# An embedding stage rewritten: centred query/key weights, one product for their norm, the embedding norm on ScalarE and the score shift inside the exponential

## The chip, the cores and the metric

The kernel runs on one core of one Trainium2 chip. The metric is the device time of one execution in microseconds (us). Names of engines are those of the profile: PE is TensorE (PEld its weight loads), DVE is VectorE, ACT is ScalarE, POOL is GpSimd, SP is SyncE, which here only issues DMAs.

## What is computed

One layer for 8 batches of 1024 tokens, width 128. For each token a row of a table is fetched (64 numbers of a fine embedding, 64 cluster logits), the logits go through a softmax and a small product, and both halves make `h`. Then attention with 8 heads, where queries and keys are normed, and a feed-forward part with a router. Cut to what the change touches:

```python
fine_emb = fine_embed_w[location_ids]
cluster_logits = loc_to_cluster_w.T[location_ids] + loc_to_cluster_b
cluster_dist = jax.nn.softmax(cluster_logits, axis=-1)
coarse_emb = jnp.einsum('bsc,ch->bsh', cluster_dist, coarse_embed_w)
h = jnp.concatenate([fine_emb, coarse_emb], axis=-1)
xn = _ln(_layernorm(h))             # two norms, one after the other
q = silu(xn) @ w_q + b_q            # k and v alike
q = _ln(q, g_q, be_q)               # k alike; (y - mean) * rsqrt(var + eps) * g + b
q = q * inner ** (-0.5)
# softmax attention over q, k, v, then the output product and the feed-forward part
```

## The kernel before

Three stages follow one another, each a block of its own with a barrier between: `embed` (about the first 254 us of the profiled execution), `attend` and `finish`. The change is in `embed` alone.

`embed` works on chunks of 512 tokens (4 tiles of 128). Four chunks, called ways, make a round, and there are four rounds (`ITERS`). Every buffer in SBUF exists once per way. The accumulators in PSUM exist twice (`SLOTS`): `psA` for transposes, `psV` for the coarse product and the values, `psQK` for queries and keys; ways 0 and 2 share one, 1 and 3 the other. Each engine runs its own list of instructions strictly in the order written by hand, and waits on semaphores that count ways. Lines below are those of the profile of before. What happens to one way:

- POOL copies the indices (L319) and issues four gathers of 128 table rows (L322), `gather`.
- ACT copies the fine half (L551). DVE adds the cluster bias (L380), finds the negated maximum (L385) and adds it (L389), all in `logits`; ACT takes the exponential of the whole way at once (L556); DVE sums it (L396, L399).
- PE transposes the exponentials (L653), ACT copies them out (L561), PE makes the coarse product (L665), DVE divides it by the sum into `h` (L407, `coarse_half`).
- DVE: mean and variance of `h` (L417, L423, L428, `stats_front`); POOL: the root (L339, `root_front`, by a power); DVE: the norm, four instructions (L435, `norm_front`); ACT: tanh (L566); DVE: silu (L443); PE transposes (L675), ACT copies out (L571, `copy_silu_t`).
- PE: bias and product with the weights (L138, L691, L696, `project`). ACT copies queries and keys from PSUM to SBUF (L578) and the values (L583), both in `copy_projected`.
- DVE: mean and variance of queries and keys (L451, L459, L462, `stats_back` and `aggregate_back`); POOL: the root (L346, `root_back`); DVE norms the queries (L468, L473, `norm_back`), ACT the keys (L591, `norm_k`), 4 instructions each.
- PE transposes them into `psQK` (L711); ACT applies gain and shift (L600) and rounds to a first bfloat16 part (L606), both in `scale_qk`; POOL subtracts that part (L354, `subtract_part0`); ACT rounds the second (L611, `round_rest`); DVE subtracts for the third (L480, `subtract_part1`). SP stores the parts, the values and `h`, and loads the first stacks for `attend`.

A round mixes two stages of the pipeline: the queries and keys of round `it` and the embedding of round `it + 1`, while POOL gathers for round `it + 2`. All rounds but the last run in a hardware loop (`Fori`) on each engine. A fifth set of gathers, for a round that does not exist (indices set to 0), is issued too, since the loop body is always the same. `regather` waits for all four ways of the round before. The work of the last round for ways 0 and 1 is split by DVE alone (L536, L538, L540).

## Time and profile before

| | us |
|---|---|
| runs of the kernel | 1194.0, 1194.92, 1200.92 (median 1194.92) |
| the profiled execution, own time | 1192.67 |
| its span | 1190.9 |
| DVE busy over the span | 983.6 (83%) |
| PE busy | 1019.2 (86%) |
| ACT busy | 762.0 (64%) |
| POOL busy | 220.5 (19%) |

The median is the number to compare with. The profiled execution is one run of the same program; the span is from its first to its last instruction, and 1.8 us lie around it. Busy time counts instructions of an engine, not whether anyone waits for them, so the stages have to be read one by one.

### The profile page before, as it was taken

What the parts mean: (1) busy time and instruction counts of PE and PEld (TensorE: products, weight loads), DVE (VectorE), ACT (ScalarE), POOL (GpSimd) and SP (SyncE); (2) the same over time, 40 slices, a digit from 0 to 9 for tenths busy, and PEclk for the clock granted to TensorE, in tenths of its full rate; (3) what the DMA queues carried; (4) which work ended last, traced back from release to release, by engine and by line L of the source; (5) the groups of instructions that cost most, each with busy time, mean ns of one, the idle gap of its engine ahead of it and who ended that gap; (6) DMA issues with size and microseconds to landing.
All of it is one profiled execution on the core that took longest, in us unless ns stands there. A gap on an engine that the chain in (4) does not pass through costs nothing. (4 is left out here: it accounts for less than half of the span.)

```text
span 1190.9 us, 30565 instructions
## 1 busy us (share of the span) xinstructions
PE 1019.2 (86%) x12144; PEld 537.1 (45%) x12144; DVE 983.6 (83%) x2004; ACT 762.0 (64%) x1414; POOL 220.5 (19%) x321
## 2 busy tenths in 40 slices
PE   0586674749999999999999999999999849897978
PEld 0474563612434444444444344444444225856556
DVE  4679798868899889989999989989898357879794
ACT  0357665722787788888888788888878935152432
POOL 6776858330000000000000000000000010202020
PEclk9976775755999999999999999999999987989899
DMA  3232857780243242432424233242300241313011
GB/s 71 69 106 95 177 124 89 159 211 7 38 79 51 41 89 38 64 66 49 81 38 73 57 55 56 58 72 38 72 12 12 89 135 38 97 53 115 8 35 36
DMA packets 81841, 85.04 MB, mean 71 GB/s; under 512 B 24241, under 2 KB 58614, under 8 KB 81718
## 3 DMA queue, kind: packets, MB, share of 16 engines
q1 hardware_dynamic: 70710, 73.87, 28.3%
q0 software_dynamic: 2560, 5.25, 3.3%
q10 hardware_dynamic: 8448, 4.20, 1.2%
q8 instruction: 88, 1.44, 0.5%
q14 instruction: 35, 0.29, 0.1%
HBM read 48.78 MB, written 34.08 MB: 70 GB/s over the span
## 5 line engine op out<-in xcount | busy, mean ns | idle before, releaser
L1089 DVE TENSOR_REDUCE b_neg_max<-psM 128x1 f32<-128x1024 f32 x512 | 603.3, 1220 | 67.3 <-PE psM L987 64.1
L1061 ACT ACTIVATE prob<-psS 128x512 f32<-128x512 f32 x1024 | 529.1, 604 | 157.5 <-PE psS L1007 157.5
L987 PE MATMUL psM<-ks,qs 96*32 96x512 bf16 x4096 | 416.0, 394 | 18.2 <-PEq L850 14.4
L1007 PE MATMUL psS<-qs,ks 99*32 99x512 bf16 x4096 | 404.9, 382 | 6.5 <-ACT prob L1061 4.5
L1021 PE MATMUL psO<-prob,vs 128*17 128x512 f32 x2048 | 266.4, 592 | 0.2 <-ACT prob L1061 0.2
L1007 PEld LDWEIGHTS psS<-qs,ks 99*32 99x32 bf16 x4096 | 114.0, 96 | 208.4 <-ACT prob L1061 103.1
L987 PEld LDWEIGHTS psM<-ks,qs 96*32 96x32 bf16 x4096 | 113.4, 97 | 176.9 <-DVE b_neg_max L1089 83.4
L882 POOL CAST mpart<-b_neg_max 128x16 bf16<-128x16 f32 x32 | 6.3, 196 | 635.1 <-DVE b_neg_max L1089 622.0
L322 POOL DMA_INDIRECT emb<-in_table,idx x80 | 79.5, 994 | 34.0 <-issue 18.3
L1021 PEld LDWEIGHTS psO<-prob,vs 128*17 128x17 f32 x2048 | 59.5, 98 | 52.0 <-ACT prob L1061 1.1
L1285 ACT ACTIVATE y_t<-c_psT 128x512 f32<-128x512 f32 x16 | 9.6, 597 | 87.6 <-PE c_psT L1345 87.6
L1377 PEld LDWEIGHTS c_psT<-w_sb,hid 128*128 128x128 f32 x512 | 59.7, 192 | 0.5
L1377 PE MATMUL c_psT<-w_sb,hid 128*128 128x128 f32 x512 | 59.8, 275 | 0.0
L675 PE MATMUL a_psA<-ident,inv_in 128*128 128x128 f32 x64 | 15.6, 425 | 44.4 <-DVE inv_in L443 41.2
L1259 POOL TENSOR_TENSOR c_rstd<-c_var_eps,neg_half 128x4 f32<-128x4 f32 x16 | 16.3, 1051 | 182.7 <-DVE c_var_eps L1444 182.7
L1367 PE MATMUL c_psF<-y_t,w_sb 128*128 128x512 f32 x64 | 40.0, 711 | 11.0 <-ACT hid L1297 11.0
L653 PE MATMUL a_psA<-ident,expo 128*64 128x128 f32 x64 | 10.8, 327 | 36.2 <-ACT expo L556 31.8
L591 ACT ACTIVATE qk<-qk,k_offset,a_rs 128x128 f32<-128x128 f32 x64 | 25.7, 481 | 17.4 <-DVE k_offset L468 17.4
L711 PE MATMUL a_psQK<-ident,qk 128*128 128x128 f32 x128 | 26.7, 383 | 11.7 <-ACT qk_full L600 10.3
L435 DVE TENSOR_SCALAR o_in<-h,a_mv,a_rs 128x128 f32<-128x128 f32 x64 | 35.7, 634 | 1.0 <-POOL a_rs L339 1.0
L451 DVE BATCH_NORM_STATS2 a_stat<-qk 128x6 f32<-128x128 f32 x128 | 26.2, 277 | 12.3 <-ACT qk L578 12.3
L1367 PE MATMUL c_psT<-y_t,w_sb 128*128 128x512 f32 x64 | 36.3, 651 | 0.0
(130 smaller groups left out, 1058.0 us busy)
## 6 DMA issues: line engine op xcount, KB each, us to landing
qk_parts<-qk_part SPq DMA_DIRECT2D x48, 256.0 KB, 3.4
qs<-qk_parts SPq DMA_DIRECT2D x192, 64.0 KB, 3.6
ks<-qk_parts SPq DMA_DIRECT2D x96, 128.0 KB, 4.3
o_cols<-ot SPq DMA_DIRECT2D x32, 256.0 KB, 4.5
qs<-mpart_t SPq DMA_DIRECT2D x384, 1.0 KB, 1.7
v_rows<-vrow SPq DMA_DIRECT2D x16, 272.0 KB, 9.6
vs<-v_rows SPq DMA_DIRECT2D x8, 544.0 KB, 5.1
h_rows<-h SPq DMA_DIRECT2D x16, 256.0 KB, 4.3
```

Of the source, the lines that this page charges most:

```text
L322: nc.gpsimd.indirect_dma_start(out=emb[w][:, t, :], out_offset=None, in_=table, in_offset=bass.IndirectOffsetOnAxis(ap=idx[w][:, t:t + 1], ...
L435: last = nc.vector.tensor_scalar(xn[w][:, t, :], h[w][:, t, :], mv[w][:, t, 0:1], rs[w][:, t:t + 1], ALU.subtract, ALU.mult)
L451: last = nc.vector.bn_stats(stat2[w][:, 2 * t + a, :], qk[w][:, t, a, :])
L591: last = nc.scalar.activation(qk[w][:, t, 1, :], qk[w][:, t, 1, :], ACT.Identity, bias=k_offset[w][:, t:t + 1], scale=rs3[w][:, 2 * t + 1: ...
L711: last = nc.tensor.transpose(psQK[w][:, a, t * P:(t + 1) * P], qk[w][:, t, a, :], c["ident"][:, :])
L987: last = nc.tensor.matmul(psM[count % MRING][q * HP:(q + 1) * HP, n, :], qs[buf][0:DATA_ROWS, half, hh, at + q * HP:at + (q + 1) * HP], ks ...
L1007: last = nc.tensor.matmul(psS[unit % SRING][q * HP:(q + 1) * HP, :], ks[buf][0:ROWS, GH * gb + hh, tile * P + q * HP:tile * P + (q + 1) * HP],
L1021: last_mm = nc.tensor.matmul(psO[HP * hh:HP * hh + VW, :], vs[buf][:, tile, GH * gb + hh, :], prob[step % PRING][:, hh, :], start=tile == ...
L1061: nc.scalar.activation(prob[step % PRING][:, hh, :], psS[unit % SRING][:, :], ACT.Exp).then_inc(score_free, 1)
L1089: nc.vector.tensor_reduce(neg_max[e % 2][:, unit:unit + 1], psM[count % MRING][:, :, :], AX.XY, ALU.max, negate=True).then_inc(max_free, 1)
L1367: nc.tensor.matmul(dst, c["w1"][:, k * P:(k + 1) * P], y_t[w][:, :], start=True, stop=True).then_inc(up_done, 1)
L1377: last = nc.tensor.matmul(psT[w][:, 1, t * DIM:(t + 1) * DIM], hid[w][:, k, t * P:(t + 1) * P], c["w2"][:, k, :], start=False, stop=t == T ...
```

## The change

Only `embed` is changed. In it:

1. Before the first round DVE subtracts from the query and key weights and biases, per row, the mean over each block of 128 output columns (new: 2 reductions and 6 `tensor_scalar`, L481 to L490 of the kernel after). The products then come out with mean zero. This and the splitting of the bias now stand behind `logits(0)` instead of ahead of it.
2. The copy of queries and keys out of PSUM (L578) is gone. DVE takes mean and variance from the accumulator itself, and one `tensor_tensor` of 128x1024 per way multiplies the accumulator by the root into SBUF (`norm_back`), in place of L468, L473 and L591.
3. The embedding norm is on ACT: four activations of 128x128 with scale and bias per partition in `tanh`. For the bias DVE writes the negated mean and POOL multiplies it by the root (`root_front`).
4. The score shift L389 is gone: ACT's exponential is four activations of 128x64 per way with the negated maximum as bias.
5. The loops are written out, `regather` waits way by way, the fifth set of gathers is gone, and `wait_apart` (a register load and two waits) is a plain wait.
6. The order is new on every engine. `project` of ways 2 and 3 now waits for `scale_qk` of ways 0 and 1, since `psQK` holds the accumulators until then; `logits` of round `it + 2` stands ahead of `stats_back` of round `it + 1`, as before, but the gathers of ways 2 and 3 for it are issued at the end of a round.

```diff
-                    for w in range(WAYS):
-                        dve.wait_ge(max_found, r * WAYS + w + 1)
-                        nc.vector.tensor_tensor(logit[w][:, :, :], logit[w][:, :, :],
-                                                neg_max[w][:, :].unsqueeze(2).to_broadcast([P, TILES, CLUSTERS]),
-                                                ALU.add).then_inc(logit_shifted, 1)
...
-                def norm_front(r):
-                    for w in range(WAYS):
-                        dve.wait_ge(rstd_done, r * WAYS + w + 1)
-                        for t in range(TILES):
-                            last = nc.vector.tensor_scalar(xn[w][:, t, :], h[w][:, t, :], mv[w][:, t, 0:1],
-                                                           rs[w][:, t:t + 1], ALU.subtract, ALU.mult)
-                        last.then_inc(xn_done, 1)
...
+                def stats_back(r, w):
+                    dve.wait_ge(qk_projected, use(r, w))
+                    for j in range(2 * TILES):
+                        last = nc.vector.bn_stats(stat2[w][:, j, :], projected(w)[:, j, :])
+                    last.then_inc(stats2_done, 1)
...
+                def norm_back(r, w):
+
+                    dve.wait_ge(rstd2_done, use(r, w))
+                    nc.vector.tensor_tensor(qk[w][:, :, :, :].rearrange("p t a n -> p (t a) n"), projected(w),
+                                            rs3[w][:, :].unsqueeze(2).to_broadcast([P, 2 * TILES, DIM]),
+                                            ALU.mult).then_inc(qk_normed, 1)
...
+                def root_front(r, w):
+                    pool.wait_ge(both_var_done, use(r, w))
+                    nc.gpsimd.tensor_tensor(rs[w][:, :], rs[w][:, :], c["neg_half"][:, 0:TILES], ALU.pow).then_inc(root_done, 1)
+                    pool.wait_ge(root_done, use(r, w))
+                    nc.gpsimd.tensor_tensor(offset[w][:, :], neg_mean[w][:, :], rs[w][:, :], ALU.mult).then_inc(rstd_done, 1)
...
+                for it in range(ITERS):
+                    last = it == ITERS - 1
+                    root_back(it, 0)
+                    regather(it + 2, 0)
...
+                def exponentials(r, w):
+                    act.wait_ge(max_found, use(r, w))
+                    for t in range(TILES):
+                        last = nc.scalar.activation(expo[w][:, t, :], logit[w][:, t, :], ACT.Exp, bias=neg_max[w][:, t:t + 1])
+                    last.then_inc(exp_done, 1)
...
+                def tanh(r, w):
+                    act.wait_ge(rstd_done, use(r, w))
+                    if r:
+                        act.wait_ge(silu_done, use(r - 1, w))
+                    for t in range(TILES):
+                        last = nc.scalar.activation(xn[w][:, t, :], h[w][:, t, :], ACT.Identity,
+                                                    bias=offset[w][:, t:t + 1], scale=rs[w][:, t:t + 1])
+                    last.then_inc(xn_done, 1)
+                    act.wait_ge(xn_done, use(r, w))
+                    nc.scalar.activation(sx[w][:, :, :], xn[w][:, :, :], ACT.Tanh, scale=0.5).then_inc(tanh_done, 1)
```

The order on POOL in the middle of a round, before (`a_rs` of 128x8 is the root for queries and keys, of 128x4 that for `h`, `emb` the gathers, `qk<-qk_full` the subtraction of the first part):

```order
L346 TENSOR_TENSOR a_rs<-a_rs,neg_half 128x8
L319 ISA
L319 COPY idx<-idx_all 128x4
L130 REGISTER_ALU
L322 DMA emb<-in_table,idx 128x128 x4
L338 ISA
L339 TENSOR_TENSOR a_rs<-a_rs,neg_half 128x4
...
L354 TENSOR_TENSOR qk<-qk_full,qk_part_0 128x1024
L354 TENSOR_TENSOR qk<-qk_full,qk_part_1 128x1024
```

And after, from the subtractions of one round's ways 0 and 1 to the middle of the next round:

```order
L353 TENSOR_TENSOR qk<-qk_full,qk_part_0 128x1024
L353 TENSOR_TENSOR qk<-qk_full,qk_part_1 128x1024
L349 TENSOR_TENSOR a_rs<-a_rs,neg_half 128x8 x2
L326 COPY idx<-idx_all 128x4
L329 DMA emb<-in_table,idx 128x128 x4
L326 COPY idx<-idx_all 128x4
L329 DMA emb<-in_table,idx 128x128 x4
L353 TENSOR_TENSOR qk<-qk_full,qk_part_2 128x1024
L353 TENSOR_TENSOR qk<-qk_full,qk_part_3 128x1024
L349 TENSOR_TENSOR a_rs<-a_rs,neg_half 128x8
L326 COPY idx<-idx_all 128x4
L329 DMA emb<-in_table,idx 128x128 x4
```

The gathers, of which three ways stood together at a round's start, now stand two and two: ways 2 and 3 ahead of the subtractions for ways 2 and 3, ways 0 and 1 each behind a root.

On DVE, the part of a round in which both norms are made, before (`h` the coarse half, `k_offset` and `qk` the norm of queries, `a_stat<-h` the statistics of `h`, `o_in` its norm):

```order
L407 TENSOR_TENSOR h<-a_psV,a_inv_sum 128x4x64
L468 SCALAR_TENSOR_TENSOR k_offset<-a_mv,a_rs 128x4
L473 TENSOR_SCALAR qk<-qk,a_mv,a_rs 128x128 x4
...
L417 BN_STATS a_stat<-h 128x6 x16
...
L435 TENSOR_SCALAR o_in<-h,a_mv,a_rs 128x128 x16
L443 SCALAR_TENSOR_TENSOR inv_in<-inv_in,o_in 128x512 x4
```

And after:

```order
L408 TENSOR_TENSOR h<-a_psV,a_inv_sum 128x4x64 x2
L455 TENSOR_TENSOR qk<-a_psQK,a_rs 128x1024 x2
L408 TENSOR_TENSOR h<-a_psV,a_inv_sum 128x4x64 x2
L418 BN_STATS a_stat<-h 128x6 x8
...
L441 BN_STATS a_stat<-a_psQK 128x6 x8
L447 BN_AGGR a_mv<-a_stat 128x2 x8
L450 TENSOR_SCALAR a_rs<-a_mv 128x8
L435 SCALAR_TENSOR_TENSOR inv_in<-inv_in,o_in 128x512 x2
```

The norm of `h` has left the list, silu (L435 after) is spread among the statistics of ways 2 and 3, and the norm of queries and keys is one instruction per way.

## Rows read from the trace of the kernel before

**Rows 1.** Windows: us, busy us (count) of each engine, granted clock, DMA share, GB/s.

```profile
64.96:113.84 48.88, 33.35 (x151) 27.82 (x152) 43.20 (x172) 34.34 (x61) 34.34 (x30) 0.65 0.26 86
113.84:166.60 52.76, 33.34 (x177) 28.49 (x177) 44.69 (x172) 34.64 (x61) 36.46 (x32) 0.71 0.62 150
166.60:218.66 52.06, 32.82 (x166) 27.88 (x165) 44.60 (x173) 32.37 (x53) 35.18 (x31) 0.67 0.71 118
218.66:249.56 30.90, 15.37 (x88) 12.96 (x86) 23.66 (x97) 23.01 (x37) 11.53 (x6) 0.76 1.00 236
```

**Rows 2.** Timeline of DVE: start us, us, instruction, [idle before <- releaser].

```profile
42.84 3.18 DVE L417 BATCH_NORM_STATS2 a_stat<-h 128x6 f32<-128x128 f32 x16
...
64.96 1.65 DVE L451 BATCH_NORM_STATS2 a_stat<-qk 128x6 f32<-128x128 f32 x8 [1.39 <-ACT qk L578]
...
131.93 0.16 DVE L468 SCALAR_TENSOR_TENSOR k_offset<-a_mv,a_rs 128x4 f32<-128x4 f32 x1 [3.57 <-POOL a_rs L346]
...
246.26 3.30 DVE L480 TENSOR_TENSOR qk_part<-qk,qk_part 128x1024 bf16<-128x1024 f32 x2 [3.10 <-ACT qk_part L611]
254.27 0.48 DVE L864 MEMSET psO<- 128x512 f32 x1 [4.71 <-PEq L313]
```

**Rows 3.** Timeline: the norm of `h` in the prologue, and in a round beside POOL's subtractions.

```profile
47.99 4.28 DVE L435 TENSOR_SCALAR o_in<-h,a_mv,a_rs 128x128 f32<-128x128 f32 x16
...
143.53 10.87 DVE L435 TENSOR_SCALAR o_in<-h,a_mv,a_rs 128x128 f32<-128x128 f32 x16 [0.50 <-POOL a_rs L339]
...
146.51 6.26 POOL L354 TENSOR_TENSOR qk<-qk_full,qk_part 128x1024 f32<-128x1024 f32 x3
```

**Rows 4.** Timeline of POOL in the second round: a way's gathers, and the roots.

```profile
118.83 0.20 POOL L319 COPY idx<-idx_all 128x4 int32 x1
119.80 0.96 POOL L322 DMA_INDIRECT emb<-in_table,idx  x1 [0.77 <-POOL idx L319]
121.07 0.94 POOL L322 DMA_INDIRECT emb<-in_table,idx  x1 [0.31 <-issue]
...
124.52 0.19 POOL L319 COPY idx<-idx_all 128x4 int32 x1
...
130.22 6.49 POOL L346 TENSOR_TENSOR a_rs<-a_rs,neg_half 128x8 f32<-128x8 f32 x4
...
142.44 4.09 POOL L339 TENSOR_TENSOR a_rs<-a_rs,neg_half 128x4 f32<-128x4 f32 x4
```

**Rows 5.** The gathers' tile `emb`: DMA times from issue to landing.

```profile
DMA to landing us min/median/max: 2.4/3.3/11.6
```

**Rows 6.** Timeline of ACT in rounds two and three.

```profile
132.13 6.46 ACT L591 ACTIVATE qk<-qk,k_offset,a_rs 128x128 f32<-128x128 f32 x16 [6.31 <-DVE k_offset L468]
138.49 1.43 ACT L600 ACTIVATE qk_full<-a_psQK,shift,gain 128x512 f32<-128x512 f32 x2
140.01 1.06 ACT L606 ACTIVATE qk_part<-qk_full 128x1024 bf16<-128x1024 f32 x1
...
158.35 3.89 ACT L611 ACTIVATE qk_part<-qk 128x1024 bf16<-128x1024 f32 x4
162.14 1.08 ACT L571 ACTIVATE h_in<-a_psA 128x512 f32<-128x512 f32 x2
163.09 1.34 ACT L551 ACTIVATE h<-emb 128x256 f32<-128x256 f32 x4
164.32 1.34 ACT L556 ACTIVATE expo<-logit 128x256 f32<-128x256 f32 x4
...
166.45 0.61 ACT L583 ACTIVATE vrow<-a_psV 128x512 f32<-128x512 f32 x1
...
168.68 1.06 ACT L561 ACTIVATE expo_t<-a_psA 64x512 f32<-64x512 f32 x2
```

**Rows 7.** Groups by shape: busy us, mean ns of one, idle before.

```profile
L1297 ACT ACTIVATE hid<-c_psF,b_sb 128x512 f32<-128x512 f32 x32 | 22.0, 687 | 12.4 <-PE c_psF L1367 12.3
L1052 ACT ACTIVATE ot<-psO 128x512 f32<-128x512 f32 x32 | 19.1, 597 | 9.9 <-PE psO L1021 9.9
```

More of the change, by code:

```diff
@@ L308, in _, with projected, use @@
                 last.then_inc(ones_set, 1)
+        def projected(w):
+            return psQK[w][:, :, :].rearrange("p b n -> p (b n)").rearrange("p (j n) -> p j n", n=DIM)
+        def use(r, w):
+            return r * WAYS + w + 1
         with nc.Block() as block:
@@ L608, in round_rest @@
-                def round_rest(r, ways_now=range(WAYS), skipped=0):
-                    for w in ways_now:
-                        act.wait_ge(rest1_done, r * WAYS + w + 1 - skipped)
-                        nc.scalar.activation(part[1][w][:, :, :], rest[w], ACT.Copy).then_inc(part1_done, 1)
-                copy_fine(0)
-                exponentials(0)
-                copy_exp_t(0)
-                tanh(0)
-                copy_silu_t(0, range(SLOTS))
-                act.wait_ge(gain_scaled, 2)
@@ new lines, in scale_qk @@
+                def scale_qk(r, w):
+                    act.wait_ge(qk_t_done, use(r, w))
+                    for a in range(2):
+                        last = nc.scalar.activation(full[w][:, a, :], psQK[w][:, a, :], ACT.Identity,
+                                                    bias=c["shift"][:, a:a + 1], scale=c["gain"][:, a:a + 1])
+                    last.then_inc(qk_scaled, 1)
+                    act.wait_ge(parts_stored[w], (r + 1) * 16 * PARTS)
+                    act.wait_ge(qk_scaled, use(r, w) + SLOTS)
+                    nc.scalar.activation(part[0][w][:, :, :], full[w][:, :, :], ACT.Copy).then_inc(part0_done, 1)
@@ new lines, in round_rest @@
+                def round_rest(r, w):
+                    act.wait_ge(rest1_done, use(r, w) - (SLOTS if r == ITERS - 1 else 0))
+                    nc.scalar.activation(part[1][w][:, :, :], rest[w], ACT.Copy).then_inc(part1_done, 1)
+                for w in range(WAYS):
+                    copy_fine(0, w)
+                for w in range(WAYS):
+                    exponentials(0, w)
+                for w in range(WAYS):
+                    copy_exp_t(0, w)
+                for w in range(WAYS):
+                    tanh(0, w)
@@ new lines, in _ @@
+                copy_silu_t(0, 0)
+                copy_silu_t(0, 1)
+                act.wait_ge(gain_scaled, 2)
+                for it in range(ITERS):
+                    last = it == ITERS - 1
+                    copy_silu_t(it, 2)
+                    copy_silu_t(it, 3)
+                    if not last:
+                        for w in range(WAYS):
+                            exponentials(it + 1, w)
+                    copy_v(it, 0)
+                    copy_v(it, 1)
+                    if not last:
+                        for w in range(WAYS):
+                            copy_exp_t(it + 1, w)
+                            copy_fine(it + 1, w)
+                    scale_qk(it, 0)
+                    scale_qk(it, 1)
+                    if not last:
+                        tanh(it + 1, 0)
+                        tanh(it + 1, 1)
+                    copy_v(it, 2)
+                    copy_v(it, 3)
+                    if not last:
+                        tanh(it + 1, 2)
+                        round_rest(it, 0)
+                        tanh(it + 1, 3)
+                        round_rest(it, 1)
+                    scale_qk(it, 2)
+                    scale_qk(it, 3)
+                    if not last:
+                        copy_silu_t(it + 1, 0)
+                        copy_silu_t(it + 1, 1)
+                    round_rest(it, 2)
+                    round_rest(it, 3)
```

602 lines of the change are left out of this document (281 added, 321 removed).

## The prediction

> **What bounds the kernel now.** I read the windows of the embedding stage first, then DVE's timeline, then POOL's and ACT's. The stage is four rounds; I mark a round by the first statistics of its queries. The marks stand at 64.96, 113.84, 166.60 and 218.66, DVE's last instruction ends at 246.26 + 3.30 = 249.56, and the next stage starts at 254.27 [rows 1, 2]. So the stage is a prologue of 65.0, rounds of 48.9, 52.8 and 52.1, a tail of 30.9, and 4.7 of last stores and barrier. No other stage is touched, so the change is worth what DVE's end of 249.56 moves.
>
> In a middle round of 52.8 DVE is busy 44.7, ACT 34.6, POOL 36.5 and PE 33.3 [rows 1]: DVE is nearest to its limit. Two things in its list can be seen. The norm of `h` takes 4.28 in the prologue and 10.87 in a round, where it runs beside three subtractions of POOL (6.26 in one piece) [rows 3]: 6.6 us of each round are DVE held up by POOL. And it waits 3.57 for POOL's root, which stands behind three ways of gathers [rows 2, 4]. POOL's busy time leaves out the pauses inside a way's gathers: a way takes 124.52 - 118.83 = 5.7, so its whole work for a round is 22.8 (gathers) + 6.5 + 4.1 (roots) + 8.3 (four subtractions of 2.09) = 41.7 [rows 3, 4]. That is nearly as much as DVE's, and the change takes nothing of it but waits.
>
> **What it does to each engine, per round.** DVE: the norm of `h` goes (-10.9, -4.3 of it proper work), the score shift goes (some -1.4), the norm of queries becomes one product of 128x1024 per way; from the subtraction in the tail (two of that size in 3.30, one held up) I take 1.2, as much as the instructions it replaces. DVE falls from 44.7 to some 33. ACT: the copies of queries and keys go (four of about 1.0), the norm of keys goes (16 in 6.46) and the norm of `h` comes (16 of the same form, 6.3) [rows 6]. The exponentials cost more: 16 of 128x64 for 4 of 128x256, which took 1.34. An activation with a bias per partition takes 687 ns where one without takes 597 [rows 7], so a pointer costs 90 ns; one of 128x128 with two pointers has a pitch of 6.46/16 = 0.40 [rows 6]; take away one pointer (0.09) and 64 columns (0.06, at (1.06 - 0.61)/512 = 0.9 ns each from the forms of 1024 and 512 columns [rows 6]) and 0.25 is left. 16 of them are 4.0. Bounds: 0.09 more (the pointer costs nothing less) 5.5, a pitch of 0.2 3.2. ACT is at about 34 as before. POOL: a small product more per way in `root_front` (1.02 becomes some 1.27, and 1.1 to 2 is possible), and a way's gathers without the apart waits 5.45 (5.2 to 5.7).
>
> The Trainium skill (page "ScalarE: Activation LUTs", section "What ACT_TABLE_LOAD costs") gives 186 ns + 0.833 ns per column, 93 ns per pointer, and an overlap of 93 ns back to back. By that the exponential would have a pitch of 0.24 and the 16 would be 3.8; the trace agrees in the pitch of the two-pointer form, which it puts at 0.386 against 0.40.
>
> **The sum: which chain sets a round afterwards.** DVE alone would allow 33 us. POOL's new order does not. From the end of `root_back` for way 3 of one round to the same of the next, with all that is waited for: two ways of gathers 10.9; subtractions for ways 2 and 3 4.2; ACT, which had to wait for them: `round_rest` 1.0, `copy_silu_t` 1.1, exponentials 4.0, two copies of values 1.2, one transposed copy 0.55, the fine copy 0.35 (8.2 in all); then POOL again: gathers of way 0 5.45 (they wait for that fine copy), root 1.65, gathers of way 1 5.45, four roots and products 5.1, two subtractions 4.2, two roots 3.3 [rows 3, 4, 6]. That is 48.4. Other engines fit in beside it by my count: DVE's statistics of `h` are ready 1 us before POOL gets to the roots, and ACT ends `round_rest` of way 1 within it.
>
> - Prologue: DVE starts the statistics of `h` at 42.84 now [rows 2]. Four ways of exponentials take 4.0 instead of 1.34, less 1.4 for the missing shift; and centring and bias splitting (about 6 us by my count of their instructions) now stand between `logits(0)` and the sums. I take 44.5. Statistics of two ways 2.7, POOL's roots until 52.6 (they need the second pair at 50.1), then gathers of ways 2 and 3 of round 1, which had waited behind the roots, 10.9, landing 1.8 (the minimum is 2.4 from issue, of which 0.94 is the instruction [rows 4, 5]), add and maximum 1.7: the first mark comes at 66.9, 1.9 later than now.
> - Round 0: exponentials until 70.0, fine copy at 72.1, then the POOL chain from way 0's gathers: 97.2. Gathers 108.1, landed 109.9, `logits` 112.6 (1 of it held up by POOL's subtractions), two remainders 3.3: second mark 115.9, a round of 49.0 against 48.9.
> - Round 1: 48.4 on POOL; third mark 164.2 (48.3 against 52.8).
> - Round 2 has no gathers in its middle, since the fifth set is gone. POOL is no longer the chain; ACT is. PE's coarse product and the transposes of way 0 are done at 177.8, then ACT in its order: two `scale_qk` of 2.5, two `tanh` with norm of 2.25, values 1.2, `tanh` 2.25, `round_rest` 1.0, `tanh` 2.25, `round_rest` 1.0, two `scale_qk` 5.0, copies 1.1, about 23; PE 3.8 to the accumulator: fourth mark 204.7 (40.5 against 52.1).
> - Tail: queries and keys stay in `psQK`, so ways 2 and 3 are projected only after `scale_qk` of ways 0 and 1, and DVE splits ways 0 and 1 (6.3) only behind its last norm. I count 33.7 against 30.9: end at 238.4.
>
> Sum: +1.9 + 0.1 - 4.5 - 11.6 + 2.8 = -11.3, and 249.56 becomes 238.3. Against the profiled execution: 1192.67 - 11.3 = 1181.4. That run lies 2.2 below the median of the runs shown, 1194.92; from the median the forecast is 1183.6.
>
> **What speaks against.** One rule of the Trainium skill bears on it (page "SBUF — State Buffer", section "Who interferes with whom"): a DVE instruction with at most one SBUF input and outside its two-port modes does not contend with POOL, one with two SBUF inputs does against POOL's reads. Rows 3 show the contention for the old norm. By the rule the new product from PSUM is free of it, while silu and the remainders are not; with 2 us of contention per round off the chain the sum is the same, with all of it on the chain it is 6 less in gain. No row of before shows the product from PSUM beside POOL.
>
> **Rivals.**
> - *More gain*: the small terms at their low ends: exponentials 3.2, gathers 5.2, PE at its full clock for the products that I took at half (granted 0.65 to 0.71 in these rounds [rows 1]), no contention. That is 0.8 + 1.0 + 0.8 in each of two rounds and about 1 in the prologue: -17, 1178. For it: most of my bounds are above the rows' pitches. Against: each step between engines costs a few hundredths that I left out.
> - *The gain is given back on POOL*: the chain of POOL keeps rounds 0 and 1 at 51 to 52 (exponentials 5.5, a product of 0.6 instead of 0.25 per way in `root_front`, gathers 5.7: +1.5 + 1.4 + 1.0 per round). Then only round 2 is shorter: 3 rounds x 3 less, a gain of 3, 1192. For it: POOL's 41.7 of work per round do not shrink. Against: 5.7 contains a wait that the change shortens.
> - *Slower, by the gathers' landing*: in three places (before the first, second and third mark) `logits` now waits for gathers issued just before, and everything of DVE and then ACT and POOL stands behind it. Now only the first has such a wait. I took 1.8; the median is 3.3 - 0.9 = 2.4, the longest 11.6 - 0.9 = 10.7 [rows 5], and the DMA engines are busy 0.62 to 0.71 in these rounds [rows 1]. At 10.7 each it is 3 x 8.9 = 27 late, less 11 of gain: +15, 1210. It decides from 3.8 us more in each place. Against: the stores of values go out 10 us earlier, and the heavy loads of the first stacks fall between 120 and 140, where no gather is waited for.
> - *The change does not do what it says on ACT*: ACT carries 16 more small exponentials and takes over the norm of `h`; if their pitch were 0.6 instead of 0.25 and 0.4, it would be the bound of every round at about 50, and the kernel within 2 us of before. The rows' pitches speak against it; it counts with the second rival.
>
> **How the numbers follow.** Forecast as above 0.50, more gain 0.20, given back 0.22, slower 0.08. A measurement of this kernel can tell about 1% (12 us) from no change. The forecast of -11.3 lies almost on that bound, so its half is split 0.26 faster, 0.24 same; more gain is all faster, given back all same. Faster 0.46, same 0.46, slower 0.08. Range: from 1174 (more gain and 4 more) to 1197 (given back, with 2 us of landing each on top), which leaves out most of the slow case and the tip of the fast one.
>
> **What would show it.** Right: marks near 67, 116, 164 and 205; the product near 1.2 us and no DVE instruction of 0.6 us per tile beside POOL's subtractions; a pitch of 0.25 for the exponentials; POOL with hardly any idle time in rounds 0 and 1 but for the wait on the fine copy; ACT with hardly any in the second half of round 2. Wrong: a round 0 or 1 below 45 (the chain on POOL is not what I think), `logits` waiting over 4 us for DMA, or a tail over 36.

## The result, and the profile after

The changed kernel takes 1190.49 us (median of 20 runs, 1185.8 to 1194.81), the kernel before 1194.88 in its 20 runs beside them: ratio 0.9963, interval 0.995 to 0.9977. That is 4.4 us faster where 11.3 were forecast, and within 1%. The profiled execution has a span of 1187.0 (1188.89 with what lies around it) against 1190.9.

The windows of the embedding stage after, cut at the four marks (first statistics of the queries) and at VectorE's last instruction; columns as in [rows 1]:

```profile
64.04:114.62 50.58, 35.36 (x183) 30.36 (x182) 35.86 (x139) 34.26 (x73) 37.36 (x36) 0.76 0.20 65
114.62:164.24 49.62, 35.45 (x172) 30.00 (x172) 35.11 (x141) 33.46 (x69) 38.03 (x36) 0.72 0.67 161
164.24:207.50 43.26, 30.80 (x143) 26.02 (x144) 30.63 (x134) 31.48 (x61) 21.93 (x16) 0.72 0.81 208
207.50:243.41 35.91, 17.43 (x97) 14.23 (x95) 28.96 (x82) 14.40 (x18) 13.47 (x6) 0.77 0.31 111
```

VectorE's timeline after, to set beside [rows 2] (start, us, and in brackets the idle time before and what ended it):

```profile
41.64 1.64 DVE L418 BATCH_NORM_STATS2 a_stat<-h 128x6 f32<-128x128 f32 x8
64.04 1.67 DVE L441 BATCH_NORM_STATS2 a_stat<-a_psQK 128x6 f32<-128x128 f32 x8
...
102.85 0.43 DVE L388 TENSOR_TENSOR logit<-emb,cluster_b_sb 128x256 f32<-128x256 f32 x1 [4.94 <-DMA emb<-in_table,idx]
108.21 2.91 DVE L388 TENSOR_TENSOR logit<-emb,cluster_b_sb 128x256 f32<-128x256 f32 x1 [4.93 <-DMA emb<-in_table,idx]
...
207.50 1.68 DVE L441 BATCH_NORM_STATS2 a_stat<-a_psQK 128x6 f32<-128x128 f32 x8 [8.40 <-PE a_psQK L709]
...
222.37 1.68 DVE L441 BATCH_NORM_STATS2 a_stat<-a_psQK 128x6 f32<-128x128 f32 x8 [4.59 <-PE a_psQK L709]
...
234.21 3.15 DVE L466 TENSOR_TENSOR qk<-qk_full,qk_part 128x1024 f32<-128x1024 f32 x1
237.39 2.49 DVE L468 CAST qk_part<-qk 128x1024 bf16<-128x1024 f32 x1
...
241.06 2.35 DVE L461 TENSOR_TENSOR qk_part<-qk,qk_part 128x1024 bf16<-128x1024 f32 x2
246.68 0.48 DVE L889 MEMSET psO<- 128x512 f32 x1 [3.26 <-PEq L321]
```

| us | before | after | forecast |
|---|---|---|---|
| prologue, to the first mark | 64.96 | 64.04 | 66.9 |
| rounds 0, 1, 2 | 48.88, 52.76, 52.06 | 50.58, 49.62, 43.26 | 49.0, 48.3, 40.5 |
| tail | 30.90 | 35.91 | 33.7 |
| VectorE's end in the stage | 249.56 | 243.41 | 238.3 |
| gap to the next stage | 4.71 | 3.27 | 4.7 |
| attention stage | 709.66 | 713.58 | unchanged |
| output and feed-forward | 226.97 | 226.74 | unchanged |

So the stage hands over 7.6 us earlier (6.15 of work and 1.44 of gap), and 3.9 of it is lost in the attention stage, whose code is not touched. All these are profiles of one execution each. How far one such profile can be trusted shows in code that an edit leaves alone: rounds 0 and 1 take 50.6 and 49.6 here, 49.3 and 50.9 in x_tail and 48.6 and 49.6 in a_pad125, and the stage of before ends at 249.56 in one profile and at 251.93 in another. So one profile does not tell a difference of 2 us or less in a round or at the stage's end from none.

### The profile page after: what moved, and what is told of

Read it like the earlier page. It is cut to its first block and busy times, and to the rows that moved or that the text cites. A ratio compares the mean times of both kernels' runs of the same rounds, so it can differ in the third digit from the quotient of the medians.

```text
span 1187.0 us, 30085 instructions
## 1 busy us (share of the span) xinstructions
PE 1024.0 (86%) x12144; PEld 545.5 (46%) x12144; DVE 953.1 (80%) x1872; ACT 756.7 (64%) x1446; POOL 211.2 (18%) x317
## 5 line engine op out<-in xcount | busy, mean ns | idle before, releaser
L329 POOL DMA_INDIRECT emb<-in_table,idx x64 | 63.3, 989 | 19.6 <-issue 14.6
L602 ACT ACTIVATE qk_full<-a_psQK,shift,gain 128x512 f32<-128x512 f32 x32 | 23.0, 769 | 36.9 <-PE a_psQK L722 36.9
L388 DVE TENSOR_TENSOR logit<-emb,cluster_b_sb 128x256 f32<-128x256 f32 x16 | 11.6, 742 | 38.7 <-DMA emb<-in_table,idx 35.1
L441 DVE BATCH_NORM_STATS2 a_stat<-a_psQK 128x6 f32<-128x128 f32 x128 | 26.7, 278 | 16.2 <-PE a_psQK L709 16.2
L722 PEld LDWEIGHTS a_psQK<-ident,qk 128*128 128x128 f32 x128 | 24.0, 212 | 33.7 <-DVE qk L455 33.4
L349 POOL TENSOR_TENSOR a_rs<-a_rs,neg_half 128x8 f32<-128x8 f32 x16 | 30.7, 1923 | 43.3 <-DVE a_rs L450 43.2
```

Source lines behind the costliest of these rows:

```text
L329: nc.gpsimd.indirect_dma_start(out=emb[w][:, t, :], out_offset=None, in_=table, in_offset=bass.IndirectOffsetOnAxis(ap=idx[w][:, t:t + 1], ...
L349: nc.gpsimd.tensor_tensor(rs3[w][:, :], rs3[w][:, :], c["neg_half"][:, :], ALU.pow).then_inc(rstd2_done, 1)
L441: last = nc.vector.bn_stats(stat2[w][:, j, :], projected(w)[:, j, :])
L602: last = nc.scalar.activation(full[w][:, a, :], psQK[w][:, a, :], ACT.Identity, bias=c["shift"][:, a:a + 1], scale=c["gain"][:, a:a + 1])
L722: last = nc.tensor.transpose(psQK[w][:, a, t * P:(t + 1) * P], qk[w][:, t, a, :], c["ident"][:, :])
```

## Experiments: does the attention stage really get longer?

**after_again and before_again**: the two kernels unchanged.

> The changed kernel once more, unchanged, to see which part of the profiled difference comes back. In the first profile the embedding stage handed over to attention 7.6 us earlier than before (246.68 against 254.27), while attention took 713.6 against 709.7 (+3.9). Theory A (the embedding stage alone changed, attention varies by chance from run to run): the hand-over is again at 246.7 +-0.5, attention falls anywhere between 708 and 715, and the ratio is 0.9935 to 0.997. Theory B (the rewritten stage makes attention longer): attention is again 713 or more.

> The kernel before once more, for a second profile: the hand-over at 254.3 +-0.5 again. Attention 709.7 again within 1 if theory B holds (its length depends on the stage before), anywhere between 708 and 715 by theory A.

after_again: 1192.2 us, ratio 0.9959 (0.9938 to 0.9979); its attention stage takes 713.55, its embedding stage ends at 243.42. before_again: one run of 1197.47, attention 711.07, and its stage ends at 251.93, since its first mark comes at 66.45 and its round 0 is 49.93. The kernel after repeats itself within 0.03 us in both stages, the kernel before does not. Against its two attention stages that of after is 2.5 to 3.9 us longer, by theory B (713 or more). The longer attention belongs to the kernel, not to chance. TensorE's timeline shows where it is, in the later half of the stage of after:

```profile
597.25 0.40 PE L1032 MATMUL psS<-qs,ks 99*32 99x512 bf16 x4 [0.55 <-DMA qs<-mpart_t]
640.35 0.40 PE L1032 MATMUL psS<-qs,ks 99*32 99x512 bf16 x4 [0.84 <-DMA qs<-mpart_t]
725.49 0.40 PE L1032 MATMUL psS<-qs,ks 99*32 99x512 bf16 x4 [0.37 <-DMA qs<-mpart_t]
768.19 0.40 PE L1032 MATMUL psS<-qs,ks 99*32 99x512 bf16 x4 [0.52 <-DMA qs<-mpart_t]
```

TensorE waits for the copies of the maxima (1 KB each, twelve a step). The waits come every 43 us or a multiple of it, that is in every second step of some 21. The slowest landing of a step does not tell these steps from the others: it is 2.5 to 3.3 us in nearly every step of before and before_again too (not 1.7, as the expectation for a_pad61 has it). What tells them apart is the issue. Where TensorE waits at 725.49 and 768.19, none of the step's twelve issues takes over 0.60 us, and yet a copy lands after 3.0 to 3.2; a landing of 3.2 without a wait in before has an issue of 1.6 us in it, so that about 1.6 is left for the copy. So at these two it is the copy itself that is late. One other thing in the profile has a fitting period: the queue that brings instructions (columns: packets, MB, share of 16 DMA engines' time):

```profile
q8 instruction: 77, 1.26, 0.9%
```

77 packets of 16 KB in 660 us are one each 8.6 us, or five in two steps, and 0.9% of 16 engines over 660 us is 1.2 us for each. TensorE issues some 3050 matmuls and weight loads in 100 us, or 262 in 8.6 us, so the queue is mostly TensorE's, with some 260 instructions to a packet; I took 256, a number that no row shows. Where a packet falls in a step then depends on how many instructions stand ahead on TensorE's list. I count 231 over a multiple of 256 in before and 170 in after (two a matmul, four where the records show an f32 product twice; a count of mine, not a row).

**Padding TensorE's list.** The edit in a_pad61, put where TensorE is idle before its first transposes (at 29.02 in after). Two waits make one instruction: the page of a_pad61 counts 30146 instructions, that of after 30085. a_pad125 has 250 waits, b_pad195 has 390 on the kernel before:

```
                 pe.wait_ge(c["weights_loaded"], 16 * len(loads))
+                for _ in range(122):
+                    pe.wait_ge(c["weights_loaded"], 16 * len(loads))
```

> The kernel after with 61 instructions more on TensorE's list, all of them waits on a semaphore that has long been reached, in the idle 15 us before TensorE's first transposes; nothing else is changed and the embedding stage should end where it did (marks 64.0, 114.6, 164.2, 207.5, hand-over 246.7). In the two profiles of after the attention stage takes 713.6 and 713.5 us, in the two of before 709.7 and 711.1, and the extra is in every second step of the second half, where TensorE waits up to 1.1 us for the copies of the maxima (qs<-mpart_t), whose landing is up to 3.5 us there against 1.7 in the same steps of before. Theory A (placement of the code): those copies collide with the 16 KB packets that bring TensorE's instructions (queue q8, one for each 256), and where these fall is set by how many instructions TensorE has ahead of the stage, which by my count is 231 over a multiple of 256 in before and 170 in after. 61 more make it 231: the attention stage back to 709.7 to 711, the span 1183 to 1184.5, ratio about 0.9935. Theory B (chance of the execution): 710 to 714, no relation. Theory C (what the embedding stage leaves behind, its DMAs or its stores): 713.5 as in after, span 1187.

> As a_pad61 with 125 instead of 61 instructions (39 over a multiple of 256). Theory A says only that the late steps move or go: another place of the fetches, so another pattern of long steps than in after, attention somewhere in 709.5 to 716. Theories B and C: 713.5 with the same steps 15 to 25 long.

> The kernel before with 195 instructions more of the same kind on TensorE's list, in its idle 17 us before the first transposes: 231 + 195 is 170 over a multiple of 256, the place of after. Theory A: the attention stage grows from 709.7 to 711 up to 713.5, with the long steps of after (every second one from the fifteenth on, 21.5 to 22.2 us), the time 2.5 to 4 us over before, ratio 1.002 to 1.0035. Theories B and C: attention 709.7 to 711 as in before, ratio 1.000.

TensorE's groups over the same stretch of the attention stage (310 to 583 us after its start) in after, a_pad61, before, b_pad195 (count, busy us, mean ns, idle before and what ended it):

```profile
L1032 PE MATMUL psS<-qs,ks 99*32 99x512 bf16 x1637 | 164.7, 381 | 2.8 <-DMA qs<-mpart_t 2.7
```
```profile
L1034 PE MATMUL psS<-qs,ks 99*32 99x512 bf16 x1652 | 163.8, 380 | 0.9 <-DMA qs<-mpart_t 0.8
```
```profile
L1007 PE MATMUL psS<-qs,ks 99*32 99x512 bf16 x1664 | 165.9, 381 | 0.0
```
```profile
L1009 PE MATMUL psS<-qs,ks 99*32 99x512 bf16 x1640 | 161.9, 380 | 2.7 <-DMA qs<-mpart_t 2.6
```

a_pad61: attention 710.23 instead of 713.58, 1185.22 us (four runs), ratio 0.9905 (0.987 to 0.9939); its own profile is its slowest run (1191.24), in which the embedding stage ends 1.6 later than in after and the last stage takes 230.9 instead of 226.7. a_pad125 (one run, 1190.78): attention 712.42, and the long steps have moved by one. Counted by GpSimd's casts of the maxima, from the second cast of one step to the first of the next, an interval is 20.4 to 20.6 us in most steps; in after the 16th, 18th and so on to the 26th have 20.7 to 21.4, in a_pad125 the 17th, 19th and so on to the 27th have 20.8 to 21.4. b_pad195: the 16th to the 26th as in after (20.9 to 21.3), attention 712.80; its time is 1201.65 us, ratio 1.005 (1.0022 to 1.0078), but 5.6 us of it are the first mark at 70.55, since the 390 waits delay TensorE's first transposes (from 31.76 to 37.37), so only the attention stage counts for the theory.

All 17 profiles of this study fall into two groups by the length of TensorE's list. Those with after's length (after, after_again, x_tail, x_fine, x_late, u_shift, u_norm, u_both) wait 2.8 to 4.3 us for these copies in this stretch, and a_pad125 and b_pad195 2.7; those with before's (before, before_again, b_norm, b_two) or with after's and 61 more (a_pad61, tail_pad61, best_late) 0.0 to 0.9. The whole attention stage is 713.0 to 714.2 in the first group and 709.4 to 711.1 in the last, with two exceptions in the first: x_late 717.75 and x_fine 719.70, whose lists on TensorE are those of after. Most of their surplus lies ahead of this stretch. In x_fine TensorE waits 1.94 us for one copy at 346.32, in a step in which one issue took 1.73, and the granted clock stands at the lower of its two levels (0.50) in the 3.1 us behind it; in x_late there is a wait of 1.41 at 390.95. So the length of TensorE's list ahead of the stage is worth 1.7 to 3.4 us of it, in both directions (a_pad61 and tail_pad61 3.4 and 3.2 less than the same kernel without the pad, b_pad195 1.7 to 3.1 more), and it is not all that makes the stage longer: in two profiles 4 to 6 us more are lost, in part to single late copies, for a reason that stays open. That the colliding thing is the instruction packet is theory A's mechanism; the period and the moved steps fit it, but no row shows a single packet beside a single late copy.

## Experiments: the embedding stage

**x_tail**: the last round's parts of ways 0 and 1 no longer wait for the last norm.

```
                     norm_back(it, 1)
+                    if last:
+                        parts_by_dve(it, 0)
 ...
-                for w in range(SLOTS):
-                    parts_by_dve(ITERS - 1, w)
+                parts_by_dve(ITERS - 1, 1)
```

> The changed kernel, but in the last round DVE splits way 0 into its parts right behind the norm of ways 0 and 1, ahead of the statistics of ways 2 and 3, and way 1 behind the last norm. Theory A (the tail is a chain on DVE's list: 6.3 us of splitting stand behind the last norm, part of it held up by POOL's subtractions): DVE ends at about 240.2 instead of 243.4, 3 us earlier, and the whole kernel is 3 us faster than the changed one. Rival (the tail is set by the last rounding on ACT and the stores): the end moves by less than 1 us.

Stage end 241.33 (-2.1, where theory A had 3 and the rival under 1), hand-over 2.0 earlier, 1188.08 us, ratio 0.9922 (0.9895 to 0.9948), which overlaps that of after_again. In after the second of these begins at 234.21, while GpSimd subtracts from 233.31 to 239.33, and takes 3.15 and 2.49 for the 1.22 and 0.69 of the first. In x_tail nothing is held, VectorE is through with them at 234.9, and the end of the tail is set by ScalarE's last rounding, which waits for GpSimd's subtractions, as it was in before:

```profile
238.02 3.31 DVE L461 TENSOR_TENSOR qk_part<-qk,qk_part 128x1024 bf16<-128x1024 f32 x2 [3.10 <-ACT qk_part L613]
```

**x_fine**: the fine halves of ways 0 to 2 are copied at the end of the round before, and each of two gathers goes ahead of its way's root.

```
-                    root_back(it, 0)
                     regather(it + 2, 0)
-                    root_back(it, 1)
+                    root_back(it, 0)
                     regather(it + 2, 1)
+                    root_back(it, 1)
 ...
+                    if it + 2 < ITERS:
+                        for w in range(3):
+                            copy_fine(it + 2, w)
```

> The changed kernel, but ACT copies the fine half of three ways as soon as they have landed (at the end of the round before, where it waits for POOL anyway), and POOL issues the gathers of ways 0 and 1 ahead of the roots instead of behind them. Theory A (rounds 0 and 1 are set by POOL's list, in which the gathers wait for the fine copy behind exponentials, values and transposed copies): the idle 6.4 us of POOL before the root are filled by gathers, rounds 0 and 1 (50.6 and 49.6) are each about 3 us shorter, round 2 stays at 43.3, the kernel is some 6 us faster than the changed one. Rival (rounds 0 and 1 are set by DVE waiting for gathers to land and then by ACT): POOL's idle time only moves, rounds change by less than 1 us.

Rounds 49.05, 49.92 and 44.46, end 243.60: no gain in the stage, as its rival had it. 1191.22 us, ratio 0.9958 (0.9937 to 0.998); the profiled run is the slowest of the eleven (1198.47), with the attention stage of 719.70 told of above. The idle time ahead of GpSimd's first root is gone, and 4.2 us of waiting for the statistics of `h` has come in its place.

**x_late**: VectorE no longer stands behind the landing of ways 2 and 3 (and ScalarE takes their exponentials behind its first two copies).

```
-                            logits(it + 2)
-                        subtract_part1(it, 0)
-                        subtract_part1(it, 1)
+                            logits(it + 2, (0, 1))
 ...
                     aggregate_back(it, 0)
+                    if it:
+                        subtract_part1(it - 1, 0)
+                        subtract_part1(it - 1, 1)
+                    if it and not last:
+                        logits(it + 1, (2, 3))
```

> The kernel after with VectorE's list changed where it waits for gathered rows: at a round's end only ways 0 and 1 get their scores, and the scores of ways 2 and 3, whose rows land 5 and 10 us later (VectorE waits 4.94 and 4.93 us for them, then 2.91 for one addition beside GpSimd's subtractions), and the two subtractions come behind the next round's first statistics; ScalarE takes the exponentials of ways 2 and 3 behind its first two copies. Theory A (that wait delays the first statistics of a round, and so GpSimd's first root, by the 6.4 us that GpSimd is idle before it): rounds 0 and 1 shorter by 3 to 6 us, 45 to 47. Theory B (the chain gathered rows, exponentials, coarse half, statistics, root is the round's real length, as moving the fine half in x_fine showed): GpSimd's idle 6.4 us goes from the first root of the round to the first root_front, and rounds stay 49 to 51.

GpSimd's waits in after and, below, in x_late:

```profile
117.25 2.59 POOL L349 TENSOR_TENSOR a_rs<-a_rs,neg_half 128x8 f32<-128x8 f32 x1 [6.42 <-DVE a_rs L450]
```
```profile
111.10 2.58 POOL L349 TENSOR_TENSOR a_rs<-a_rs,neg_half 128x8 f32<-128x8 f32 x1 [0.48 <-DVE a_rs L450]
118.30 0.18 POOL L326 COPY idx<-idx_all 128x4 int32<-128x4 int32 x1 [4.61 <-ACT h L567]
...
161.66 2.58 POOL L349 TENSOR_TENSOR a_rs<-a_rs,neg_half 128x8 f32<-128x8 f32 x1 [1.47 <-DVE a_rs L450]
171.56 1.64 POOL L349 TENSOR_TENSOR a_rs<-a_rs,neg_half 128x8 f32<-128x8 f32 x1 [7.32 <-DVE a_rs L450]
179.06 1.01 POOL L343 TENSOR_TENSOR a_rs<-a_rs,neg_half 128x4 f32<-128x4 f32 x1 [5.85 <-DVE a_rs L429]
```

The root comes 6.2 us earlier, but the gather behind it starts at 118.30 instead of 119.81: its wait is now for the fine copy. The marks that both orders share (way 2's statistics) go from 133.72 and 184.12 to 133.25 and 182.26, and the stage ends at 245.64, 2.2 later, since the tail grows from 35.9 to 39.1. The one run takes 1195.46 us. By this profile it is theory B: nearly all of the idle time was slack in a closed chain, as in x_fine. That the wait is worth nothing at all does not follow; best_late below has the same edit and ends its stage earlier.

**u_shift, u_norm, u_both**: one part undone, or two. In u_shift the shift is a VectorE pass again; in u_norm VectorE normalizes `h` again:

```
-                    act.wait_ge(max_found, use(r, w))
-                    for t in range(TILES):
-                        last = nc.scalar.activation(expo[w][:, t, :], logit[w][:, t, :], ACT.Exp, bias=neg_max[w][:, t:t + 1])
+                    act.wait_ge(logit_shifted, use(r, w))
+                    last = nc.scalar.activation(expo[w][:, :, :], logit[w][:, :, :], ACT.Exp)
 ...
```
```
-                        last = nc.scalar.activation(xn[w][:, t, :], h[w][:, t, :], ACT.Identity,
-                                                    bias=offset[w][:, t:t + 1], scale=rs[w][:, t:t + 1])
 ...
+                            last = nc.vector.tensor_scalar(xn[w][:, t, :], h[w][:, t, :], mv[w][:, t, 0:1],
+                                                           rs[w][:, t:t + 1], ALU.subtract, ALU.mult)
```

> The kernel after with one part undone: the shift of the scores is a pass of VectorE again (four instructions of 128 x 256 a round, 0.43 us each) and the exponential one ScalarE instruction of about 1.34 us for each way instead of four of 0.25. Marks of after to compare: 64.0, 114.6, 164.2, 207.5. Theory A (the shift lay on the chain from the landing of the gathers to the next statistics): 1.4 us more of ScalarE and 1.7 of VectorE stand on it, so rounds 0 and 1 each 1.5 to 3 us longer (52 to 53.5), prologue 2 to 3 longer. Theory B (hidden behind GpSimd's list): rounds 0 and 1 within 0.5 us of 50.6 and 49.6, and only the prologue longer. Attention stage 713.5 either way, as TensorE's list is as long as that of after.

> The kernel after with one part undone: the embedding norm is VectorE's again (16 instructions of 128 x 128 a round, 4.3 us where nothing runs beside them, 10.9 beside GpSimd's products and gathers in before), so ScalarE has 6.5 us less a round, GpSimd 0.8 less. Theory A (as my prediction had it: in round 2 ScalarE is the bound, in rounds 0 and 1 GpSimd's chain): round 2 gets 1 to 4 us shorter than 43.3, rounds 0 and 1 change by less than 1. Theory B (VectorE, stretched by GpSimd's work, is again what the round waits for): rounds 0 and 1 longer by 3 to 6, round 2 longer by 1 to 4. Attention stage 713.5.

> The kernel after with two parts undone at once (score shift and embedding norm on VectorE again, as in u_shift and u_norm): what is left of the change is the centred weights, the one product from the accumulators, and the order of the lists. u_shift ended the embedding stage 3.4 us later than after, u_norm 11.4, together more than the 6.15 us that the whole change took from the stage (249.56 to 243.41). Theory A (the parts add up): end at 243.41 + 3.4 + 11.4 = 258.2, so the third part by itself makes the stage 8 to 9 us longer than before's 249.6. Theory B (the two undone parts hide behind each other): end at 254 to 256. Only an end at or under 249.6 would say that the third part gains, as my prediction had it.

**b_norm, b_two**: the same parts put into the kernel before, first the norm, then norm and shift; lists and loops stay before's.

> The kernel before with one part of the change: the embedding norm on ScalarE (four activations of 0.41 us for each way, offset by one small product on GpSimd of 0.2 us, one small VectorE operation more). Lists otherwise in before's order. Theory A (this is the part that gains, VectorE being what a round waited for): stage ends 8 to 12 us earlier than 249.6, rounds of 52.8 and 52.1 become 49 to 50. Theory B (ScalarE, 33 us of each round already, or before's order of the lists takes the gain): 0 to 3 us. Attention stage 709.7 to 711, as TensorE's list is before's.

> The kernel before with two parts of the change, the embedding norm on ScalarE and the score shift in the exponential, and without the centred weights. Theory A (the third part costs 8 to 9 us, since the accumulators are held through statistics, root, product, transposes and scaling, so that the projections of ways 2 and 3 start later): the stage ends at 235 to 238, before's last part of 30.9 us is kept, span 1176 to 1180, ratio 0.986 to 0.990, better than after. Theory B (the third part gains or is even): the stage ends at 243.4 or later, ratio 0.994 to 1.000.

Seven of the eight combinations; the shift alone on the kernel before was not run. What is called the third part is all the rest of the change at once: centred weights, the product from the accumulators, the written-out loops, and the new order of the lists. Each row is one profile. The busy times are those of the round from the second to the third mark:

| kernel | norm | shift | third part | stage ends | that round | VectorE | ScalarE |
|---|---|---|---|---|---|---|---|
| before | | | | 249.6 | 52.8 | 44.7 | 34.6 |
| b_norm | x | | | 250.3 | 52.3 | 39.6 | 40.9 |
| b_two | x | x | | 249.4 | 51.6 | 37.6 | 43.3 |
| u_both | | | x | 256.9 | 55.6 | 43.4 | 24.4 |
| u_norm | | x | x | 254.8 | 54.2 | 41.7 | 27.1 |
| u_shift | x | | x | 246.8 | 52.4 | 39.2 | 30.8 |
| after | x | x | x | 243.4 | 49.6 | 35.1 | 33.5 |

Windows of b_two and of u_both that the table draws on:

```profile
118.89:170.53 51.64, 33.59 (x176) 28.15 (x175) 37.64 (x156) 43.34 (x89) 36.50 (x37) 0.74 0.62 152
```
```profile
120.86:176.42 55.56, 32.89 (x175) 28.11 (x174) 43.38 (x158) 24.44 (x42) 36.71 (x32) 0.75 0.59 144
```

The single runs take 1195.57 (u_shift), 1203.46 (u_norm), 1202.24 (u_both) and 1194.65 us (b_norm). u_norm is theory B (rounds 53.9, 54.2, 46.7: 3.3 to 4.6 longer each). u_shift is between its theories: prologue +2.1, round 0 -1.1, round 1 +2.7, round 2 -0.1. b_norm and b_two miss theory A: no gain at all (b_two: 1197.01 us, ratio 1.0001, 0.9984 to 1.0018), and so theory B of b_two. u_both ends at 256.9, between its theories (258.2, and 254 to 256), and far from the 249.6 below which the third part would gain by itself: alone it costs 7.3 us (5.0 against the end of before_again); beside norm and shift the same part gains 6.0 (249.4 to 243.4). The parts do not add up, they need each other: between having and not having the other two, the third part's worth turns by 13.3 us, far more than two profiles of one kernel differ. The 0.2 and 0.7 of b_two and b_norm are not told from nothing. Norm and shift take 7 us a round off VectorE and put 8.7 on ScalarE, and b_two's round is only 1.1 shorter for it. The third part takes 10 us off ScalarE (43.3 to 33.5), but alone leaves the norm of `h` on VectorE, in a chain that now also runs through the held accumulators. That the tenure of the accumulators is the 7.3 us is argued from the waits (ScalarE's waits for TensorE's query and key transposes sum to 57.3 us in u_both), not shown: there is no PSUM left to try a second set, and the order of the lists was never changed by itself.

**Versions that beat both.** tail_pad61 is x_tail with 61 instructions more on TensorE's list, best_late adds x_late:

> The two findings together: the last round's parts of the first ways begun right behind their products (as in x_tail) and the 61 instructions of a_pad61. Theory A: embedding stage 2.0 us shorter than after, attention 710 to 711 instead of 714.2, span 1181.5 to 1183, ratio to before 0.989 to 0.991. Theories B and C: as x_tail, 0.992.

> x_late, the early parts of x_tail and 61 instructions more on TensorE's list, together. If x_late gains its 3 to 6 us in a round: embedding stage ends at 232 to 237, attention 710 to 711, span 1172 to 1178, ratio 0.980 to 0.986. If it gains nothing: as tail_pad61, 1184.6, ratio 0.991.

tail_pad61: 1184.58 us, ratio 0.991 (0.9884 to 0.9936), stage end 242.46, hand-over 245.85, attention 710.98, as theory A had it; against a_pad61 (245.01) the early parts are worth 2.5 of the stage's end, against the 2.1 of x_tail. best_late: its profile has the lowest span, 1178.1 (stage end 239.33, attention 711.04, last stage 224.3), but it is the fastest of four runs from 1179.85 to 1189.38 with a median of 1187.28, ratio 0.9927 (0.9901 to 0.9953). Its stage ends 3.1 us ahead of tail_pad61's, which differs from it by x_late's edit alone: with the last parts split early, the same edit that cost 2.2 above gains 3.1. One profile each does not settle which of the two is its worth. The intervals of a_pad61, tail_pad61 and best_late overlap; they are 9 to 11 us faster than before.

## Why the prediction was right and wrong, by its steps

The forecast of -11.3 missed in two places. The embedding stage was to end at 238.3 and ended at 243.4: the prologue came 2.9 early, the rounds 1.6, 1.3 and 2.8 late, and the tail took 2.2 more. The attention stage then took 3.9 more, and the shorter gap gave 1.4 back.

- **The small prices held.** Exponentials 3.93 us for 16 (forecast 4.0), the product from PSUM 1.21 to 1.23 (1.2), roots with products 1.24 a way (1.27), gathers 5.3 a way (5.45), landing 1.6 after the last issue (1.8).
- **The sum's step "No other stage is touched, so the change is worth what DVE's end moves" failed.** From the same end the gap shrank by 1.44 and the attention stage grew by 3.9. The stage's code is the same; what stands ahead of it on TensorE's list is not, and a_pad61 takes 3.4 of it back with nothing but that list made longer.
- **Prologue, forecast +1.9, measured -0.9.** Statistics of `h` start at 41.64, not 44.5: centring and splitting fitted beside the exponentials and TensorE's coarse product. The rest followed, and the mark came 2.9 early too.
- **Rounds 0 and 1, forecast 49.0 and 48.3, measured 50.6 and 49.6.** GpSimd's own links were right, but "Other engines fit in beside it by my count" was not: twice VectorE, held up by GpSimd's subtractions, let GpSimd wait.

```profile
86.37 4.94 DVE L435 SCALAR_TENSOR_TENSOR inv_in<-inv_in,o_in 128x512 f32<-128x512 f32 x2 [0.66 <-ACT inv_in L585]
93.87 2.01 POOL L349 TENSOR_TENSOR a_rs<-a_rs,neg_half 128x8 f32<-128x8 f32 x1 [1.06 <-DVE a_rs L450]
118.03 0.41 ACT L564 ACTIVATE h<-emb 128x256 f32<-128x256 f32 x1
119.81 0.18 POOL L326 COPY idx<-idx_all 128x4 int32<-128x4 int32 x1
```

  In round 0 two silu of 0.69 each take 4.94 beside the subtractions, way 3's statistics come late by it, and the last two roots take 5.15 with their wait, not 3.3. At the second mark, from the end of the subtractions (110.83) to the next gather (119.81) it takes 9.0 and not 8.2, and it is not the fine copy through ScalarE that ends it (118.44), but GpSimd's root. That root waited 6.42 us for VectorE, whose addition of 0.43 had taken 2.91, and itself took 2.59 and not 1.65. x_late moves it out of the way, and the gather waits for the fine copy, as forecast, 1.5 earlier. Two subtractions took 4.66 to 5.10 and not 4.2. VectorE is busy 35.1 to 35.9 in these rounds where 33 were forecast.
- **Round 2, forecast 40.5, measured 43.3.** ScalarE's leg began 1.4 late (179.18 against 177.8), and the way from its last copy to the mark took 4.9 (202.6 to 207.5) instead of 3.8.
- **Tail, forecast +2.8, measured +5.0.** Direction and place were right: projections of ways 2 and 3 behind the accumulators (VectorE waits 8.40 and 4.59 for them), and the parts split last. Too small was the price of the split, 6.3: the cast and subtraction stretched beside GpSimd are 3.7 over, and x_tail, which takes them from there, returns 2.1.
- **The rivals.** "Slower by the landing" named a wait of more than 4 us for DMA as the sign; the waits of 4.9 are there, but VectorE was only early for rows that landed on time, and taking the wait off its list gave nothing in x_late and 3.1 at the stage's end in best_late, so its price stays open. "Given back on POOL" is nearest to the outcome in size (1192), and that is partly luck: the measured rounds 0 and 1 lie between it and the forecast, but its prices for the exponentials (5.5) and the product on GpSimd (0.6) did not come, and 3.9 of what was given back were lost in a stage that no rival named. The working of the prediction, part by part, hid the strongest fact of the study: neither norm and shift nor the third part gained without the other.
- **The two-input rule of the Trainium skill** (page "SBUF — State Buffer", section "Who interferes with whom"): a VectorE instruction with two SBUF inputs contends with one of GpSimd that reads SBUF, one with at most one, outside its two-port modes, does not. The trace agrees for the forms that it names as contending. The addition and the subtraction with two SBUF inputs were held (0.43 became 2.91, 1.22 became 3.15), and so was the cast (0.69 became 2.49). That section of the Trainium skill says of a cast that it can enter a two-port mode, and so contend. The 6.3 of my tail is twice 1.22, 0.69 and 1.23, with none of them held. The product from PSUM shows 1.21 to 1.23 wherever it stands alone, beside GpSimd's roots too (at 143.72, beside 142.06 to 145.30), but no row of it lies beside a subtraction of GpSimd, so its own exemption was not put to the test. The statistics, which read PSUM alone, were: those at 140.04 take 1.67 as elsewhere, while GpSimd subtracts from 137.00 to 142.10.

## What to carry to other kernels

Price a rewrite not by its parts but by the pair of engines that it moves work between: here a part that unloaded one engine was worth nothing until another part gave the next one room, and most of an idle stretch in a closed chain was slack, not gain. Where two engines run side by side, price the instruction that is held, and ask who waits for it. When an untouched stage changes its length, compare waits of its DMAs step by step, and pad the longest instruction list ahead of it (here by 61 instructions) before looking for another cause. Work with no deadline (here the split of the last parts) should not be left to stand beside the other engine's last long instruction.

## What the runs showed of the hardware that I had not expected

- The number of instructions ahead on TensorE's list changes a later stage by 1.7 to 3.4 us of 710, in both directions. In after itself the stage repeats within 0.03 us (713.58, 713.55), but x_late and x_fine, with the same list there, have 717.75 and 719.70.
- Very small VectorE instructions can be held as long as two of GpSimd's large ones. In u_both, where VectorE's 128x8 operation takes 0.17 us elsewhere:

```profile
142.42 4.01 DVE L461 TENSOR_SCALAR a_rs<-a_mv 128x8 f32<-128x8 f32 x1
```
```profile
142.20 4.20 POOL L352 TENSOR_TENSOR qk<-qk_full,qk_part 128x1024 f32<-128x1024 f32 x2
```

  A 128x256 addition is held in the same way (0.43 alone, 2.91 at 108.21, while GpSimd subtracts from 106.62 to 110.83).
- Still open: the last stage takes 224.3 to 230.9 us in profiles of kernels that share its code, without an order that I could see, and a_pad61's embedding stage ends 1.6 us later than after's though its first four marks agree within 0.25.
